# A first list of tiles made from a running tally, and a new order of the first loads and router products, in a one-core attention and mixture-of-experts kernel

## Time and profile before

| what | us |
|---|---|
| median of 3 runs (lowest, highest) | 425.51 (423.96, 427.02) |
| the profiled execution, device time | 424.67 |
| its span, first to last instruction | 422.9 |
| its mean granted TensorE clock | 0.988 of full speed |

### The profile page before, as it was taken

The page is one execution under the profiler, slowest core; times in us unless marked ns, Lnnn a source line. Parts: engine busy times, 40 slices in busy tenths (PEclk is TensorE's granted clock), DMA queues, the critical chain, the costliest instruction groups (busy, mean ns, idle before and its releaser), DMA issues.

```text
span 422.9 us, 14560 instructions
## 1 busy us (share of the span) xinstructions
PE 403.4 (95%) x3446; PEld 387.8 (92%) x3446; DVE 281.1 (66%) x1674; ACT 323.8 (77%) x830; POOL 321.0 (76%) x606
## 2 busy tenths in 40 slices
PE   8999999999997999999999999999999999999980
PEld 7968899998896999999999999999999999999980
DVE  2444899999999667556565555446766667666662
ACT  1228799999897688777887887888788888888851
POOL 7000189888889888888888787748888888788885
PEclk9999999999998999999999999999999999999996
DMA  9999611111115523545544555643333343423211
GB/s 228 316 403 390 136 48 44 47 47 48 42 55 150 110 61 91 134 139 138 148 118 124 134 146 150 162 118 90 109 96 105 112 107 105 109 84 108 65 33 37
DMA packets 45490, 51.69 MB, mean 122 GB/s; under 512 B 6610, under 2 KB 37074, under 8 KB 45410
## 3 DMA queue, kind: packets, MB, share of 16 engines
q1 hardware_dynamic: 37312, 31.46, 28.1%
q0 software_dynamic: 7728, 18.51, 13.0%
q10 hardware_dynamic: 370, 0.80, 0.6%
HBM read 28.23 MB, written 21.72 MB: 118 GB/s over the span
## 4 chain that ended last, share of the span: by engine, by line
PE 47%; POOL 27%; issue 11%; DVE 6%; SPq 4%; DMA 3%; ACT 1%; POOLq 1%; DVEq 0%
PE bank L877 17%; PE bank L892 17%; POOL queue L583 11%; POOL idle L567 5%; POOL r_z L611 5%; POOL out L617 4%; PE bank L694 3%; PE bank L867 2%; PE bank L685 2%; DMA x_all<-x 1%; SPq L442 1%; POOL queue L604 1%; DVE x_all L1266 1%; SPq L435 1%; SPq L444 1%
## 5 line engine op out<-in xcount | busy, mean ns | idle before, releaser
L877 PE MATMUL bank<-xT 128*128 128x128 f32 x1136 | 152.0, 277 | 0.0
L892 PE MATMUL bank<-w2T,xT 128*128 x1136 | 150.3, 275 | 0.4 <-DVE yt L1440 0.4
L892 PEld LDWEIGHTS bank<-w2T,xT 128*128 128x128 f32 x1136 | 138.3, 192 | 0.6 <-issue 0.6
L877 PEld LDWEIGHTS bank<-xT 128*128 128x128 f32 x1136 | 138.7, 193 | 0.0
L929 ACT ACTIVATE xT<-w1T,zero_col 128x512 f32 x139 | 100.4, 722 | 41.7 <-issue 36.6
L1440 DVE TENSOR_TENSOR yt<-bank,b_bc 128x128 f32<-128x128 f32 x142 | 41.5, 292 | 88.4 <-PE bank L892 78.4
L617 POOL DMA_INDIRECT out<-xT,xg x71 | 75.8, 1067 | 16.8 <-issue 16.5
L604 POOL DMA_INDIRECT queue<-xT,xg x71 | 72.1, 1016 | 17.6 <-POOL idle L602 13.7
L1070 ACT ACTIVATE xT<-bank 128x512 f32<-128x512 f32 x142 | 82.1, 578 | 2.2 <-PE bank L877 2.2
L583 POOL DMA_INDIRECT queue<-x_all x64 | 62.2, 972 | 11.5 <-issue 6.7
L929 ACT ACTIVATE xT<-bank,one_col 128x128 f32<-128x128 f32 x142 | 52.1, 367 | 11.5 <-PE bank L867 5.6
(11 more groups left out here) (227 smaller groups left out, 727.2 us busy)
## 6 DMA issues: line engine op xcount, KB each, us to landing
xg<-queue SPq DMA_DIRECT2D x71, 129.5 KB, 2.2
xg<-queue SPq DMA_DIRECT2D x71, 67.5 KB, 2.4
x_all<-x SPq DMA_DIRECT2D x16, 256.0 KB, 6.1
xT<-x_t SPq DMA_DIRECT2D x8, 512.0 KB, 9.9
w1r<-w_t SPq DMA_DIRECT2D x8, 256.0 KB, 5.9
w2T<-w_t SPq DMA_DIRECT2D x8, 256.0 KB, 11.5
queue<-xT,xg POOLq DMA_INDIRECT x71, 2.7
out<-xT,xg POOLq DMA_INDIRECT x71, 2.4
```

The lines of the kernel that those rows point to most:

```text
L877: last = mm(bank[2 + s][:, h * P:(h + 1) * P], w1c[:, (q - 1) % WR, h * P:(h + 1) * P], xgT[:, s, :], start=True, stop=True)
L892: last = mm(bank[4 + s][:, 0:P], hs[:, s, h, :], w2T[:, bass.ds(e, 1), h, :].rearrange("p a d -> p (a d)"), start=(h == 0), stop=(h == HC ...
```

## The change

1. The first list. PE's tally after batch 17 is what the reduce over one-hots counted. DVE reads it in step 22 on one partition (`n0_row`, with the queue bases taken off and a division by 128), and PE spreads it by a product with one row of ones at step 23. The list starts at step 24 (`LIST0_AT`) and takes parts 0 to 6: floor and ceiling come from adding -127/256 or +127/256 and 2^23 and taking 2^23 off again; the table look-up is a single compare, since `look` holds differences instead of values. PE's `spread_table` and DVE's `take_table` stay at steps 28 and 30. The second list's division is made in the same way, with as many instructions.
2. The start. ACT loads its table of functions first and issues the small loads only when chunk 1 of x has landed. Round 0 stands after chunk 6, round 1 after chunk 10.
3. The two products of the router's bias stand after the last Gram product, and DVE copies them after it has copied `wp2T`.

```diff
-            ROUND_AFTER_CHUNK = {4: 0, 9: 1}
+            ROUND_AFTER_CHUNK = {6: 0, 10: 1}
...
-                    mm(bank[2][:, 3 * P + E:3 * P + 2 * E], rlb_bc[:], rwT, start=True, stop=False)
-                    mm(bank[2][:, 3 * P + E:3 * P + 2 * E], ones[0:1, :], rb[:], start=False, stop=True)
...
             last.then_inc(s_gram, 1)
+            mm(bank[1][:, 0:E], rlb_bc[:], rwT, start=True, stop=False)
+            mm(bank[1][:, 0:E], ones[0:1, :], rb[:], start=False, stop=True).then_inc(s_rbias, 1)
...
+            act.preload_act_table_set("natural_log_exp_and_others")
+            act.wait_ge(s_x[1], 16)
             act.dma_start(low_s[:], low).then_inc(s_small, 16)
             act.dma_start(wide_s[:], wide).then_inc(s_small, 16)
             act.dma_start(rb[:], r_b.unsqueeze(0)).then_inc(s_small, 16)
-            act.preload_act_table_set("natural_log_exp_and_others")
...
-                    op(v.tensor_copy(r_bias[:], bank[2][:, 3 * P + E:3 * P + 2 * E]))
...
             op(v.tensor_copy(wp2T[:, 0:E], bank[2][:, 3 * P + 2 * E:3 * P + 3 * E]))
+            v.wait_ge(s_rbias, 1)
+            op(v.tensor_copy(r_bias[:], bank[1][:, 0:E]))
...
-                if known == COUNT0:
+                if known == COUNT0 + 2:
                     pe.wait_ge(s_wc, E)
                     pe.wait_ge(s_n0, 1)
-                    mm(bank[6][:, 0:2 * E], ones_h[:], n0_h[:], start=True, stop=True).then_inc(s_n0t, 1)
+                    mm(bank[6][:, 0:2 * E], ones[0:1, :], n0_row[:].rearrange("p k e -> p (k e)"), start=True,
+                       stop=True).then_inc(s_n0t, 1)
...
+                    if b4 == NB0:
+                        v.scalar_tensor_tensor(out=n0_row[:], in0=rkb[0:1, 0], scalar=1.0 / P, in1=base_row[:],
+                                               op0=ALU.mult, op1=ALU.subtract).then_inc(s_n0, 1)
...
                 if n == 0:
-                    pg.settle()
-                        v.tensor_reduce(n0_h[:], oh_all[:, 0:NB0 * TPB].rearrange("p t k e -> p (k e) t"),
-                                        AXX, ALU.add).then_inc(s_n0, 1)
-                if n == 2:
                     v.wait_ge(s_n0t, 1)
-                    op(v.tensor_copy(n0[:].rearrange("p c e -> p (c e)"), bank[6][:, 0:2 * E]))
-                if n in range(3, 14):
-                    pg.settle(listed[0])
-                if n == 3:
-                    op(v.tensor_copy(tiles_i[:, FULL], n0[:]))
-                    op(v.tensor_scalar(tiles_i[:, UP], n0[:], P - 1.0, None, ALU.add))
-                if n == 4:
-                    op(v.tensor_scalar(tiles_s[:, FULL:ALL], tiles_i[:, FULL:ALL], P.bit_length() - 1, None,
-                                       ALU.logical_shift_right))
-                if n == 5:
-                    op(v.tensor_copy(tiles[:, FULL:ALL], tiles_s[:, FULL:ALL]))
+                    counts = bank[6][:, 0:2 * E].rearrange("p (c e) -> p c e", c=2)
+                    op(v.tensor_scalar(halves[:, FULL], counts, -BELOW, WHOLE, ALU.add, ALU.add))
+                    op(v.tensor_scalar(halves[:, UP], counts, BELOW, WHOLE, ALU.add, ALU.add))
+                if n in range(1, 7):
+                    pg.settle(listed[0])
+                if n == 1:
+                    op(v.tensor_scalar(tiles[:, FULL:ALL], halves[:], -WHOLE, None, ALU.add))
+                if n == 2:
+                    spread_parts(0)
+                    op(v.tensor_scalar(look[:, 0, :, 0, 1:E + 1], tiles[:, FULL], -float(P), float(CAP), ALU.mult, ALU.add))
                 if n == 3:
...
```

More of the change, by code:

```diff
@@ L296, in build @@
         s_scat = [sem("s_scat0"), sem("s_scat1")]
-        n0_h = sb("n0_h", [P, 2 * E], F16)
-        n0 = sb("n0", [P, 2, E])
+        n0_row = sb("n0_row", [1, 2, E])
+        base_row = sb("base_row", [1, 2, E])
+        halves = sb("halves", [P, 2, 2, E])
+        BELOW, WHOLE = 127.0 / 256, 2.0 ** 23
         base = sb("base", [P, 2, 2, NPART])
         FULL, UP, ALL = range(3)
-        tiles_i, tiles_s = sb("tiles_i", [P, 3, 2, E], I32), sb("tiles_s", [P, 3, 2, E], I32)
+        raised = sb("raised", [P, 2, E])
         tiles = sb("tiles", [P, 3, 2, E])
@@ L350, in build @@
         COUNT0 = NB0 + 3
+        LIST0_AT = COUNT0 + 3
         LATE_GE = 2
@@ L504, in _ @@
                 last = PARTS[g] - 1
[L505 to L509, removed]
+                if g == 0:
+                    pg.did(pool.iota(look[:, 0, :, 0, 0:1], [[0, 2], [0, 1]], base=0, channel_multiplier=P,
+                                     allow_small_or_imprecise_dtypes=True))
+                    pg.did(pool.memset(look[:, 0, :, 1, 1:last], 1.0))
+                    pg.did(pool.memset(look[:, 0, :, 1, 0:last + 1:last], 0.0))
+                else:
+                    pg.did(pool.iota(look[:, g, 0, 1, 0:last], [[0, g + 1], [1, E]], base=0, channel_multiplier=0,
+                                     allow_small_or_imprecise_dtypes=True))
+                    pg.did(pool.iota(look[:, g, 1, 1, 0:last], [[0, g + 1], [1, E]], base=0, channel_multiplier=0,
+                                     allow_small_or_imprecise_dtypes=True))
+                    pg.did(pool.memset(look[:, g, :, 1, last:last + 1], E - 1.0))
                 pg.did(pool.memset(base[:, g, :, last:last + 1], float(DUMMY)))
@@ L517, in _ @@
             pg.did(pool.memset(eps_1[:], EPS_POST * EPS_FFN))
+            pg.did(pool.iota(base_row[:], [[0, 2], [CAP // P, E]], base=0, channel_multiplier=0,
+                             allow_small_or_imprecise_dtypes=True))
             pg.did(pool.iota(j_iota[:], [[NTILE0, 2]], base=0, channel_multiplier=1, allow_small_or_imprecise_dtypes=True))
@@ L1259, in attend_step @@
                     row_max(k)
[L1260 to L1261 removed]
+                if known >= LIST0_AT:
+                    list_first_group(2 * (known - LIST0_AT))
                 if has[2]:
@@ L1355, in list_first_group @@
                 if n == 0:
-                    pg.settle()
-                    with nc.allow_low_precision(reason="whole numbers up to NT"):
-                        v.tensor_reduce(n0_h[:], oh_all[:, 0:NB0 * TPB].rearrange("p t k e -> p (k e) t"),
-                                        AXX, ALU.add).then_inc(s_n0, 1)
+                    v.wait_ge(s_n0t, 1)
+                    counts = bank[6][:, 0:2 * E].rearrange("p (c e) -> p c e", c=2)
+                    op(v.tensor_scalar(halves[:, FULL], counts, -BELOW, WHOLE, ALU.add, ALU.add))
@@ L1365, in list_first_group @@
                 if n == 3:
-                    op(v.tensor_copy(tiles_i[:, FULL], n0[:]))
-                    op(v.tensor_scalar(tiles_i[:, UP], n0[:], P - 1.0, None, ALU.add))
+                    op(v.tensor_tensor(cmp[:, 0, :, 0:E + 1], j_iota[:, 0:1].unsqueeze(1).to_broadcast([P, 2, E + 1]),
+                                       start[:, 0, :, 0:E + 1], ALU.is_ge))
                 if n == 4:
-                    op(v.tensor_scalar(tiles_s[:, FULL:ALL], tiles_i[:, FULL:ALL], P.bit_length() - 1, None,
-                                       ALU.logical_shift_right))
+                    op(v.tensor_tensor(picked[:, 0, :, :, 0:E + 1],
+                                       cmp[:, 0, :, 0:E + 1].unsqueeze(2).to_broadcast([P, 2, 2, E + 1]),
+                                       look[:, 0, :, :, 0:E + 1], ALU.mult))
@@ L1371, in list_first_group @@
                 if n == 5:
-                    op(v.tensor_copy(tiles[:, FULL:ALL], tiles_s[:, FULL:ALL]))
+                    sum_part(0)
+                listed[0] = pg.n
                 if n == 6:
[L1374 to L1384, removed]
@@ L1404, in list_second_group @@
                     ends = bank[7][:, 0:2 * E].rearrange("p (c e) -> p c e", c=2)
-                    op(v.scalar_tensor_tensor(out=tiles_i[:, ALL], in0=ends, scalar=P - 1.0, in1=first,
+                    op(v.scalar_tensor_tensor(out=raised[:], in0=ends, scalar=P * BELOW, in1=first,
                                               op0=ALU.add, op1=ALU.subtract))
@@ L1412, in list_second_group @@
                     v.sem_inc(s_pad, 1)
-                    op(v.tensor_scalar(tiles_s[:, ALL], tiles_i[:, ALL], P.bit_length() - 1, None,
-                                       ALU.logical_shift_right))
+                    op(v.tensor_scalar(raised[:], raised[:], 1.0 / P, WHOLE, ALU.mult, ALU.add))
                     op(v.tensor_tensor(used[:], reach[:, :, 1:E + 1], reach[:, :, 0:E], ALU.subtract))
                 if n == 2:
-                    op(v.tensor_copy(tiles[:, ALL], tiles_s[:, ALL]))
+                    op(v.tensor_scalar(tiles[:, ALL], raised[:], -WHOLE, None, ALU.add))
                     op(v.tensor_tensor(count[:, :, 0, :], tiles[:, UP], used[:], ALU.subtract))
```

10 lines of the change are left out of this document (3 added, 7 removed).

## The result

The changed kernel takes 426.79 us (median of 20 runs, 425.64 to 429.21) against 425.43 (20 runs, 423.86 to 427.06) for the kernel before: a ratio of 1.0035, interval 1.0022 to 1.0048. I had forecast 424.8. The time lies in the range, and far within 1% of no change, but on the other side: 1.4 us slower, where I had forecast 0.7 faster. The interval leaves out 1.

A forecast was written before the change was run, and what follows sets the result against it. Bound: PE up to 45 us, then POOL's scatters and SP's loads until tile 29 at 192.08, then PE. Profiled 424.67 less 0.7 (start), list 0, gave 424.0; that execution lying 0.84 below the median, forecast 424.8, range 421.7 to 427.0.

The forecast's parts named there:

- the part on the list: First list, attention steps 21 to 26: 2.1 us saved on PE and DVE, POOL not moved, 0 at the end.
- The list's saving: DVE's attention steps: old list costs 3.5 us, new one 1.35; 2.1 us saved, bounds 1.2 and 2.8.
- the wait for PE's product: DVE at step 24, waiting for a product of step 23: costed at nothing.
- Worth nothing at the end: Before tile 29: the list's 2.1 us end in PE's idle time, 3.3 us instead of 1.2; value 0.
- rival A: Attention: the list's time comes through because POOL and SP aren't the bound, 2.8 us in all, 422.7; chance 0.13.
- The start: Loads and Gram products: 0.8 us sooner less 0.1 for the bias products, 0.7 passed on whole.
- The step with the small loads: Start: small loads issued from 5.1 us are there at 11.4, before round 0 at 12.5.
- rival D: Start gives nothing: small loads beside x take 8 us instead of 6.2 and round 0 waits; 425.5, chance 0.13.
- Rival B: TensorE's clock falls before tile 29 after PE's waits in tiles 22 to 29: 1.7 us lost, 426.5; chance 0.12.
- Rival E: Whole kernel: its own spread decides, three runs differing by 3.1 us, more than any other rival; no chance given.

The follow-up runs named there:

- a4: The changed kernel as it is, run once more for a second profile: 426.81 us, ratio 1.0045 to the kernel before.
- group a: First four follow-up kernels (new list alone, new start alone, changed with loads at once, changed again), timed with the kernel before, whose median there was 424.47 us.
- c1: The kernel before with the new list alone and without the unused iota of part (602 POOL instructions): 437.54 us, ratio 1.0007.
- a1: The kernel before with the new first list alone; loads, rounds and bias products as before: 427.36 us, ratio 1.0055.
- b1: The kernel before with one small memset more in POOL's preparation (603 instructions): 439.06 us, ratio 1.0052.
- c3: The kernel before with one small memset more in POOL's preparation, second run: 440.32 us, ratio 1.0057.
- d3: The kernel before with one small memset more in POOL's preparation, third run: 440.08 us, ratio 1.004.
- a2: The kernel before with the new start alone (table first, late small loads, moved rounds and bias products) and the old list: 424.21 us, ratio 0.9982.
- a3: The changed kernel with ACT's small loads issued at once, ahead of the table load: 426.55 us, ratio 1.0047 to the kernel before.
- b2: The changed kernel without POOL's unused iota of part (602 instructions): 437.04 us, ratio 0.9984 to the kernel before.
- b3: The changed kernel with one small memset more on POOL (604 instructions): 437.5 us, ratio 0.9991 to the kernel before.
- b4: The changed kernel with small loads at once and without the iota of part (602 POOL instructions): 436.3 us, ratio 1.0004 to the kernel before.
- d2: The kernel before with the new list alone, 602 POOL instructions, and no spare-tile memset ahead of each scatter but the first: 459.38 us, ratio 1.045.
- e1: The kernel before with one small memset more on POOL, put behind batch 0's two scatters (603 instructions): 444.84 us, ratio 0.9992.
- e2: The kernel before with two small memsets more in POOL's preparation (604 instructions): 445.59 us, ratio 1.0012.
- c4: The changed kernel without POOL's unused iota of part (602 instructions), second run: 438.41 us, ratio 0.9995 to the kernel before.
- c2: The changed kernel with small loads at once and without the iota of part (602 POOL instructions), second run: 437.97 us, ratio 1.0005.
- d4: The changed kernel with small loads at once and without the iota of part (602 POOL instructions), third run: 437.33 us, ratio 0.9963.
- groups b, c and d: Later sets of follow-up kernels, each timed with the kernel before, whose median there was 437.03, 437.99 and 437.93 us.
- d1: The kernel before without POOL's spare-tile memset ahead of each scatter but the first: 460.51 us, too spread for a ratio.

## Why the prediction was wrong

**The step that failed** is in the part on the list: "They don't move POOL: its first scatter is at step 4, and the list starts at 22." The DVE instructions of the list don't. But an instruction in POOL's preparation comes ahead of every scatter, and I gave it no line in the sum at all. By its own duration it is free: POOL stands idle for 23.96 us before its first memset. What it did was to shift the first scatter by one place, and that costs 2.72 less 0.52, 2.2 us in a4, on the chain that passes a delay on whole to tile 29 in the profiles of this kernel and of group a. I had read that chain rightly, and then used it only to argue that savings vanish; I didn't ask what could lengthen it.

**The sum for a4**, whose start was undisturbed. POOL's first memset is 0.84 us sooner (50.39 against 51.23), the stall adds 2.2, the way to tile 29 takes 0.3 more (140.22 against 139.92), together 1.7, as 193.75 less 192.08 says. Behind tile 29 it took 0.85 more (231.65 against 230.8, span less tile 29). That makes 2.5, the difference of the spans (425.4 against 422.9); timed in group a, 2.3. Behind tile 29 the two profiles of the kernels with the old list have 230.7 and 230.8 and the four with the new one 231.1 to 231.65; these 0.3 to 0.95 us stay open. If they belong to the list, they are a second and smaller loss that I had no term for; the timings of the list with 602 (c1, 1.0007) can't tell.

**The list's saving: right in direction, 2.1 was 1.3.** DVE's marks of steps 20 and 28 in a4:

```profile
91.99 0.62 DVE L1282 SCALAR_TENSOR_TENSOR x_all<-bank,rinv,x_all 128x136 f32<-128x136 f32 x2
...
116.67 0.62 DVE L1282 SCALAR_TENSOR_TENSOR x_all<-bank,rinv,x_all 128x136 f32<-128x136 f32 x2
```

24.7 us for eight steps against 26.0; without a list I had them at 22.5. So the new list costs 2.2, and I had counted 1.35. Three of DVE's instructions in it:

```profile
103.55 0.17 DVE L1377 TENSOR_SCALAR halves<-bank 128x16 f32<-128x16 f32 x1 [0.21 <-PE bank L856]
...
105.74 0.55 DVE L1382 TENSOR_SCALAR tiles<-halves 128x32 f32<-128x32 f32 x1
...
107.22 0.62 DVE L1385 TENSOR_SCALAR look<-tiles 128x16 f32<-128x16 f32 x1
```

The first of them, which reads PE's bank, takes 0.17 us; the other two, from and to SBUF, take 0.55 and 0.62 for 32 and 16 columns. Reading from SBUF alone doesn't make them slow: the old list had an instruction of the same kind, 16 columns from SBUF with integers as output, in 0.17 us (L1367, at 101.69), and one of 32 columns, integers to integers, in 0.66 (L1369, at 102.70). So the new list has two of the slow sort where the old one had one; what makes them slow wasn't tried. I had priced the small ones as a fraction of the parts of the earlier trace rows, all alike; and the wait for PE's product that I had at nothing is 0.21.

**Worth nothing at the end: right.** The first expert tile came 2.2 us sooner on PE (128.28 against 130.50), 0.84 of it by the start, and tile 29 came no sooner for it. PE's stretches in a4 from 160 to 200 us:

```profile
160.00:170.00 10.00, 8.79 (x79) 8.61 (x78) 5.61 (x27) 6.85 (x15) 8.86 (x25) 1.00 0.32 99
170.00:180.00 10.00, 9.40 (x81) 8.90 (x80) 5.46 (x27) 7.46 (x14) 8.85 (x26) 1.00 0.49 139
180.00:190.00 10.00, 8.60 (x69) 7.87 (x70) 5.08 (x26) 6.29 (x12) 8.87 (x26) 1.00 0.47 137
190.00:200.00 10.00, 8.01 (x68) 7.66 (x68) 5.40 (x30) 5.57 (x11) 8.86 (x27) 1.00 0.49 130
```

Its busy times leave 5.2 us idle (40 less 34.80). The kernel before has 1.2 there, its last stretch being:

```profile
190.00:200.00 10.00, 9.16 (x82) 8.95 (x81) 6.18 (x34) 7.28 (x14) 8.85 (x25) 1.00 0.49 136
```

I had forecast 3.3; the saving as measured (1.4), the start's 0.84, by which PE came sooner still, and the 1.7 us by which tile 29 came later make 1.2 + 1.4 + 0.84 + 1.7 = 5.1. This sum must come out if PE's busy time from its first expert tile to tile 29 is the same in both, and it is: 59.2 us. It says where the saving went, and isn't a test of its own. The timed pairs don't speak against it: the list alone at an equal number of POOL's instructions gives 1.0007 with 602 (c1), and with 603 it is 1.0055 (a1) beside 1.0052, 1.0057 and 1.004 for the kernel before with 603 (b1, c3, d3). But these are timings of different groups, and the interval of c1 reaches down to 0.9977, 1.0 us less. So rival A falls by the profiles of group a, in which all of the saving goes into waiting. The kernel in which POOL's chain is shorter, and the saving would show, I didn't get.

**The start: 0.7 forecast, 0.5 to 1.2 measured** at POOL's first memset (50.73 in a2, 50.07 to 50.39 in a3, a4, b2, b3 and b4, against 51.23), and 0.9982 timed for a2, whose interval reaches 1. The old start spreads too: 50.75 to 51.09 in b1, c3, d2, e1 and e2. In a4 the Gram products ended at 22.91 (18.28 + 4.63), where I had 22.92. The step with the small loads was off, though. PE in a2, on chunk 6 and at round 0:

```profile
10.77 1.16 PE L693 MATMUL bank<-x_all 128*128 128x129 f32 x8 [0.46 <-DMA x_all<-x]
12.90 0.93 PE L664 MATMUL bank<-low_s 64*128 64x128 f32 x6 [0.97 <-DMA rb<-r_b]
```

The loads were there at 12.2 to 13.8 in the profiles in which round 0 waited for them (after, a2, b2, b3 and c4), not at 11.4 as forecast, and round 0 waited 0.46 to 1.79 us (0.46 in c4, 1.79 in the changed kernel's profile). That is rival D's mechanism; the start kept its gain all the same, except in the changed kernel's own profile, where the lower clock followed. In a4 round 0 found the loads there, and PE waited 1.03 us for chunk 6 instead, where I had 0.6. Issuing them late gained nothing over issuing them at once: a3 and a4 have 1.0047 and 1.0045, and the same first memset within 0.1.

**Rival B did not come**: the clock is 1.00 in all four stretches above, and in each stretch of 5 us of a4 from 120 to 230 us, though PE was busy for only 3.27 of 5 us in 190 to 195. In the earlier trace rows the clock was 0.77 with 3.78 of 5 us; a2 had 3.70 in that same stretch, 130 to 135, and the clock was 1.00. So the busy time of one such stretch doesn't tell whether the clock falls, and B's comparison of 3.78 with 4.17 had too little to stand on. **Rival E** was too strong: single runs spread by 3 us, but 20 of each tell 1.4 us from nothing.

**A version that beats both?** The changed kernel with the loads at once and 602 instructions measured 1.0004, 1.0005 and 0.9963 (b4, c2, d4). Two of the three intervals hold 1, so it recovers the loss and isn't shown to be better than the kernel before; it ran only in groups with the longer times. There the profiles show PE, not POOL, as the chain in attention. By the account above the stall should then have cost less or nothing, yet b1, c3 and d3 lost the same 0.4 to 0.6% by their timings. So the added instruction by itself is shown to cost the time (groups b, c and d), and the way by which the stall reaches the end only in group a.

## What to carry to other kernels

An instruction that is free by its duration isn't free by that alone: list every instruction that a change adds ahead of the first step of the binding chain, on each engine, and after the change read the idle time before that step first. A small difference that shows far upstream of the code that the change was about can come from where instructions stand in a stream, and not from what they do. A dummy instruction added to the kernel before, and one taken from the kernel after, tell the two apart in two runs. And where a chain swallows savings whole, ask what would lengthen it: here it passed a delay on whole.

## What the runs showed of the hardware

- One POOL instruction more ahead of the first indirect DMA makes that DMA begin 2.2 to 2.4 us later (2.72 to 2.92 us of idle in place of 0.52), two more don't, and one more behind it doesn't. The instruction may do anything (a memset or an `iota`). The trace calls the idle time "issue". An 8 KB packet of the instruction queue q14 begins inside the idle time in all seven such profiles and in none of the thirteen others; that POOL waits for it is likely and wasn't tested.
- The small loads (541 KB) took 6.2 us when issued at the start, with x beside them, and 9.1 us when issued at 4.72 behind two chunks of it (landed at 13.78, the after kernel), 7.6 in another execution of the same kind (b2, 4.59 to 12.21).
- The granted clock fell in the Gram products of some executions and not of others: 0.66 for 5 us in the profiled run of the changed kernel, 1.00 in a4's of the same kernel. It isn't tied to the new start: c1, d1 and d3, with the old one, had 0.73 or 0.74 in 5 to 10 us. In these four PE had just stood idle for 1.38 to 1.79 us at one go; in the other sixteen no wait in the Gram products was longer than 1.03 us. From c1:

```profile
7.03 5.48 PE L706 MATMUL bank<-x_all 128*128 128x129 f32 x32 [1.48 <-DMA x_all<-x]
```

- Passes can be slow without a lower clock in the profile: in a1 the same 32 took 6.79 us, 0.21 each, and the first eight of the earlier trace rows 0.25 each, both with the granted clock given as 1.00. What slowed them stays open:

```profile
7.59 6.79 PE L707 MATMUL bank<-x_all 128*128 128x129 f32 x32 [0.58 <-DMA x_all<-x]
```

- Taking 0.43 us of memset from between POOL's scatters, which made POOL's part lighter, made the kernel 5% slower (460.51 us in place of 437.93).
